# Rounding a quantised activation: the magnitude by a bit mask on VectorE, the subtraction on GpSimd

## What is computed

```python
def _div_clamp_fp8(x, scale):
    y = jnp.clip(x.astype(jnp.float32) / scale, -FP8_MAX, FP8_MAX)   # 448
    y = y.astype(jnp.bfloat16).astype(jnp.float32)
    return _fp8_roundtrip(y)                                          # float8_e4m3fn
def _fp8_linear_pertensor(x, wq, w_scale, in_scale):
    xq = _div_clamp_fp8(x, in_scale)
    return jnp.einsum('bsi,oi->bso', xq * in_scale, wq) * w_scale
...
ln_out = _ln(hidden_states, ln_w, ln_b)
q  = _fp8_linear_pertensor(ln_out, wq,  wq_scale,  q_in_scale)
k  = _fp8_linear_pertensor(ln_out, wk,  wk_scale,  k_in_scale)
v  = _fp8_linear_pertensor(ln_out, wv,  wv_scale,  v_in_scale)
qx = _fp8_linear_pertensor(ln_out, wqx, wqx_scale, qx_in_scale)
```

## Time and profile before

| | |
|---|---|
| median of 3 runs | 1316.26 us (1315.24 to 1320.13) |
| the profiled execution | 1319.29 us, its span 1317.5 us |
| mean granted TensorE clock | 0.986 of full speed |
| busy, share of the span | TensorE 94%, VectorE 84%, ScalarE 75%, GpSimd 54% |
| the chain that ended last | TensorE 75%, VectorE 11%, ScalarE 5%, DMA 3%, GpSimd 2% |
| pieces of the rounding | 32, the first begins at 15.7 us, the last ends at about 135 us |

### The profile page before, as it was taken

How to read it: one execution, slowest core, us unless ns; L and a number is a source line. 1 busy time by engine, 2 the same in 40 slices (tenths; PEclk the granted TensorE clock), 3 DMA queues, 4 the chain that set the end, 5 groups by cost and what they waited for, 6 DMA issues and landing times.

```text
span 1317.5 us, 28707 instructions
## 1 busy us (share of the span) xinstructions
PE 1237.3 (94%) x10612; PEld 1089.1 (83%) x10612; DVE 1100.4 (84%) x2220; ACT 982.3 (75%) x2186; POOL 705.5 (54%) x614
## 2 busy tenths in 40 slices
PE   1688999999999999999999999999999999998998
PEld 1578899999999999999999999987877545555998
DVE  8989879999989999989999988986666768876654
ACT  5799788789987889898789897755433456674775
POOL 5667555656656657556565564433210346664585
PEclk9989999999999999999999999999999999998999
DMA  4222332231132321223321111221186703125762
GB/s 149 83 73 68 97 93 77 75 92 50 56 87 63 96 76 48 71 76 74 89 66 43 34 37 28 75 75 39 29 150 149 148 27 74 47 98 188 254 230 78
DMA packets 117513, 114.02 MB, mean 87 GB/s; under 512 B 12411, under 2 KB 102491, under 8 KB 116768
## 3 DMA queue, kind: packets, MB, share of 16 engines
q1 hardware_dynamic: 115152, 106.11, 29.3%
q0 software_dynamic: 2048, 6.05, 1.3%
q10 hardware_dynamic: 176, 0.04, 0.0%
HBM read 80.20 MB, written 32.00 MB: 85 GB/s over the span
## 4 chain that ended last, share of the span: by engine, by line
PE 75%; DVE 11%; ACT 5%; DMA 3%; issue 3%; POOL 2%; SPq 0%; POOLq 0%; DVEq 0%; ACTq 0%
PE PC L599 8%; PE PO L581 7%; PE SS L565 7%; PE B L542 5%; PE PA L498 4%; PE PA L500 4%; PE B L1319 3%; PE B L1850 2%; PE PA L512 2%; PE PA L511 2%; PE PC L589 2%; PE PA L510 2%; PE PO L1300 2%; PE B L555 2%; PE PA L523 2%
## 5 line engine op out<-in xcount | busy, mean ns | idle before, releaser
L1093 POOL TENSOR_TENSOR RB<-YS,M 128x512 bf16<-128x512 f32 x128 | 162.5, 1270 | 309.7 <-DVE YS L928 309.7
L718 ACT ACTIVATE QT<-B,sm 128x256 f32<-128x256 f32 x256 | 131.9, 571 | 43.5 <-PE B L542 43.4
L498 PE MATMUL PA<-WH,XQ 128*128 128x256 f32 x512 | 140.4, 306 | 17.4 <-DVE WL L874 13.3
L1088 POOL TENSOR_TENSOR yy<-vv,half 128x14 f32<-128x14 f32 (+1 forms) x64 | 148.4, 2318 | 5.3
L565 PE MATMUL SS<-QT,KT 128*128 128x256 f32 x512 | 132.9, 382 | 3.1 <-DVE mx L878 3.1
L500 PE MATMUL PA<-WL,XQ 128*128 128x256 f32 x512 | 129.6, 285 | 0.0
L741 ACT ACTIVATE PPP<-SS 128x512 f32<-128x512 f32 x128 | 77.7, 607 | 68.7 <-PE SS L568 68.6
L898 DVE TENSOR_TENSOR QN<-QN,yy 128x512 f32<-128x512 f32 x128 | 127.1, 993 | 0.8 <-POOL yy L1088 0.8
L890 DVE TENSOR_REDUCE vv<-SQ 128x7 f32<-128x896 f32 (+1 forms) x128 | 120.7, 943 | 0.4 <-ACT SQ L764 0.3
L498 PEld LDWEIGHTS PA<-WH,XQ 128*128 128x128 f32 x512 | 98.7, 193 | 18.9 <-DVE WL L874 13.7
L542 PE MATMUL B<-identf,QN 128*128 128x128 f32 x768 | 106.2, 275 | 2.0 <-ACT LNT L673 1.0
(11 more groups left out here) (369 smaller groups left out, 4148.4 us busy)
## 6 DMA issues: line engine op xcount, KB each, us to landing
W<-in_w SPq DMA_DIRECT2D x16, 1024.0 KB
XK<-xk_d SPq DMA_DIRECT2D x24, 512.0 KB, 4.3
V<-v_d SPq DMA_DIRECT2D x112, 64.0 KB
v_d<-VST SPq DMA_DIRECT2D x48, 128.0 KB, 2.3
Q<-qsc SPq DMA_DIRECT2D x8, 768.0 KB, 10.2
WR<-in_wprojT SPq DMA_DIRECT2D x16, 256.0 KB, 3.0
xk_d<-XK SPq DMA_DIRECT2D x8, 512.0 KB, 3.9
kt_d<-KT SPq DMA_DIRECT2D x64, 64.0 KB, 1.7
```

Source lines behind the costliest of these rows:

```text
L498: pe.matmul(PA[:, 256 * k:256 * k + 256], XQ[:, k, c, bs], wh[:, c, 256 * k:256 * k + 256], start=c == 0, stop=False)
L718: a.activation(QT[i % 2][:, o:o + 256], B1[:, o:o + 256], ACT.Identity, bias=col(n + "b"), scale=col(n + "w"))
L1088: p.tensor_tensor(yy[j % 2][:, :, 0:n], v_, half[:, 0:2 * n].rearrange("p (h k) -> p h k", h=2), ALU.pow).then_inc(s_rstd, 1)
L1093: p.tensor_tensor(RB[i % 2][:], YS[:], M[:], ALU.subtract).then_inc(s_rb, 1)
```

## The change

ScalarE makes only QY, now scaled by `scq`, so `scn` goes, and `s_qm` becomes `s_qy`. VectorE clears the sign bit of QY to get QM, clamps QY in place, bounds QM from both sides, and adds 2^-20 QY to QM. GpSimd subtracts QM from the sum, which leaves the rounded value; it no longer clamps. The final operation of a piece on GpSimd so has two tensor inputs in place of one.

```diff
-        scn = sb("scn", [128, 4, 2])
...
-                    a.wait_ge(s_qm, 8 * q4)
+                    a.wait_ge(s_qy, 8 * q4)
...
-            a.activation(QY[i % 3][:], LNT[:, c], ACT.Copy, scale=scn[:, k, c:c + 1])
-            if i >= 2:
-                a.wait_ge(s_qs, i - 1)
-            a.activation(QM[i % 2][:], LNT[:, c], ACT.Abs, scale=scq[:, k, c:c + 1]).then_inc(s_qm, 1)
+            a.activation(QY[i % 3][:], LNT[:, c], ACT.Copy, scale=scq[:, k, c:c + 1]).then_inc(s_qy, 1)
...
-            v.wait_ge(s_qm, i + 1)
+            v.wait_ge(s_qy, i + 1)
             if i >= 2:
                 v.wait_ge(s_q, i - 1)
-            v.scalar_tensor_tensor(out=s_[:], in0=m[:], scalar=QMIN, in1=y[:], op0=ALU.max, op1=ALU.add).then_inc(*vs.up())
-            v.wait_ge(*vs.at())
-            v.scalar_tensor_tensor(out=s_[:], in0=m[:], scalar=QMIN, in1=s_[:], op0=ALU.max, op1=ALU.subtract).then_inc(s_qs, 1)
+            v.tensor_scalar(m[:].bitcast(U16), y[:].bitcast(U16), 0x7FFF, None, ALU.bitwise_and).then_inc(*vs.up())
+            v.tensor_scalar(y[:], y[:], QMAX, -QMAX, ALU.min, ALU.max)
+            v.wait_ge(*vs.at())
+            v.tensor_scalar(m[:], m[:], QMIN, QMAX, ALU.max, ALU.min).then_inc(*vs.up())
+            v.wait_ge(*vs.at())
+            v.scalar_tensor_tensor(out=s_[:], in0=y[:], scalar=1.0 / TWO20, in1=m[:], op0=ALU.mult, op1=ALU.add).then_inc(s_qs, 1)
...
-                v.tensor_scalar(scn[:, k, :], scq[:, k, :], -1.0, None, ALU.mult).then_inc(*vs.up())
...
-            p.tensor_scalar(dst, QS[i % 2][:], 448.0, -448.0, ALU.min, ALU.max).then_inc(s_q, 1)
+            p.tensor_tensor(dst, QS[i % 2][:], QM[i % 2][:], ALU.subtract).then_inc(s_q, 1)
```

More of the change, by code:

```diff
@@ L227, in build @@
         s_zv = sem("zv")
-        s_qturn, s_lnt, s_qm, s_qs, s_q = (sem(n) for n in ("qturn", "lnt", "qm", "qs", "q"))
+        s_qturn, s_lnt, s_qy, s_qs, s_q = (sem(n) for n in ("qturn", "lnt", "qy", "qs", "q"))
         s_c, s_ch, s_ctx = (sem(n) for n in ("c", "ch", "ctx"))
```

## The result

The changed kernel takes 1328.9 us in the median of 6 runs (1326.4 to 1330.6), the kernel before 1317.0 us beside it (6 runs, 1315.2 to 1320.1): a ratio of 1.0085, with a 95% interval of 1.0068 to 1.0103, or +11.9 us. The forecast was 1326.5 us, +10.2 us.

A forecast was written before the change was run, and what follows sets the result against it. Chain before turn 12: VectorE and GpSimd to 59 us, then mostly ScalarE, with VectorE level and becoming the bound. Terms 2.4 + 1.7 + 2.3 - 0.6 + 4.7 - 0.3 = +10.2 us gave 1326.5 us; 80% range 1314 to 1335.

The forecast's parts named there:

- It passes one for one to the end: Behind turn 11 TensorE has the same work and no idle time, so any shift before turn 12 reaches the end.
- The level costs: Lengths without holds, per piece: VectorE 1.36 us instead of 1.33; GpSimd's subtraction at least 1.147 us instead of 0.608.
- The hold: VectorE standing behind a GpSimd subtraction loses 0.54 us more than before; bounds 0 and 0.86 us.
- To 28.2 us: Before the first projection: GpSimd's longer pieces delay VectorE and share ports with pieces 2 and 3, +2.4 us.
- To 59: From the start to 59 us, through piece 11 and the reload of CR: 2.4, 1.7 and 2.3 us more.
- the four scn products: Four products dropped by the change, each on the chain with 0.07 us: together -0.3 us.
- Turns 3 to 5: Turn 3 +0.6 with VectorE full, turn 4 0, turn 5 -1.2 from ScalarE's two removed instructions: sum -0.6 us.
- the rival of a late GpSimd: GpSimd also becomes a bound, adding 1 to 2 us in each of turns 6, 8 and 10: 1332 us, chance 0.12.
- Turns 6 to 11: VectorE becomes the bound: 2.4 us in turns 7, 9, 11 and 3.4 in 6, 8, 10, less idle time: 4.7 us.
- the prediction's first rival: ScalarE's relief comes through: VectorE stays level, twelve L686 leave the chain, -7.3 us, 1309.0 us; chance 0.09.

## Why the prediction was right

*The bound and the place.* "It passes one for one to the end": 12.4 us at block 12, 11.9 between the medians. The other runs say the same, each with one trace: the sum of squares of block 12 lies 1.8 us earlier than in the kernel before with the one-input form of before, and 7.6, 11.5 and 15.3 later with two inputs in the kernel before, with VectorE's subtraction, and with subtraction and clamp exchanged; the ratios give -2.4, +8.4, +10.4 and +14.9 us. The farthest apart are those of the changed kernel with the sum of squares moved in turns 5 to 11, 13.4 against 10.3. One for one is shown to within some 3 us, not closer.

*The level costs.* VectorE's estimate of 1.36 us a piece holds: in turn 7 the two masks of a pair start 1.33 us apart, 103.45 and 104.78. GpSimd's at least 1.147 us came as 1.152.

*The hold.* "Where VectorE stands behind a subtraction, I take 0.54 us more": measured 1.0 instead of 0.29 where a mask precedes, 0.71 more, nearer to the upper bound of 0.86. Over all pieces it is 0.5 us. The term is right in the sum and a little small per place: 0.16 us of it is what a hold gains by the short instructions, as estimated above. It also falls elsewhere than was said: not the first instruction of a second piece, the mask, but the clamp behind it is held, and so often that its median is 0.72 us and not 0.29.

*To 28.2 us*: +2.4 forecast, +2.4 measured. *To 59*: 6.4 forecast (6.1 with the scn products), CL ended 6.7 later. The -0.3 us for the four scn products did not come: the first statistics start no earlier, since VectorE's reciprocal ahead of them then waits for the transfer of the smoothing factors instead.

*Turns 3 to 5*: forecast -0.6, measured +1.3 (8.0 less 6.7). This is the step that failed: "in turn 5 ScalarE's two removed instructions come through". The three scalings of weights on GpSimd (L1027) took 4.70 us in place of 2.83, with VectorE's rounding of two pieces now beside them, where before only the start of one was; the root behind them came late, and ahead of the scaling of the queries at 82.22 VectorE stood idle for 1.9 us; that scaling was then held for 1.0 by the next subtraction. That is the rival of a late GpSimd, in one turn and at 2 us; I had looked for it in turns 6, 8 and 10.

*Turns 6 to 11*: forecast 4.7, measured 4.4 from turn 6 to block 12 (12.4 less 8.0).

*The rivals.* In the changed kernel ScalarE's relief is worth 0.4 to 1.6 us, far from the 7.3 us that its twelve places on the chain of before suggested. That is no verdict on the 7.3 us in the kernel before. With the one-input form of before the whole is 2 us faster although VectorE's pieces are held 7 us more, and with two inputs in the kernel before, where they are also held 7 us more (17 against 10) but ScalarE has no relief, it is 8 us slower. The distance of 10 us between these two is an upper estimate of what the relief pays as long as VectorE is held for no more than that; they differ also in the length of GpSimd's step. No run has the relief alone, so between 2 and some 10 us its worth there stays open, and the prediction's first rival may have had a real gain in it that the two-input form used up.

The Trainium skill, "SBUF — State Buffer", section on the two separate sides, says that the shared port pair is held for the whole instruction. The subtraction agrees roughly (1.0 us of hold for 1.15), the product with a minimum does not: 0.45 us of hold for 1.92. By the rule that run's pieces would have held VectorE for about as long as GpSimd was busy; the measurement decides. The same clamp L843 was held for 0.45 us by one-input instructions of 0.61 and of 1.92 us and for 1.0 us by the two-input one of 1.15 us, and L848 for 0.29 us by one input and 0.72 by two. So the hold looks more like the tensors read than the length; why, no run shows.

## What to carry to other kernels

Work moved to an engine with idle time is free only if it leaves the bound engine alone: price a GpSimd instruction by what it does to VectorE's instructions beside it, and look for two-input forms in particular. Splitting one long VectorE instruction into short ones gives GpSimd more openings, and the same neighbour then held VectorE for longer (0.45 us instead of 0.29). Where two engines are level, what the relief of one is worth can depend on how far the same change loads the other; a run with the relief alone tells.

## What was not expected of the hardware

- On GpSimd a one-input instruction with a product and a minimum on 128x512 took 1.92 us, with a minimum and a maximum 0.61 us.
- That 1.92 us instruction held VectorE for 0.45 us only, and two further VectorE instructions, one of them with two tensor inputs, ran beside it without a hold. Of all VectorE instructions that began beside one of the 32, none was held for more than 0.47 us.
- VectorE holds GpSimd as well: three scalings of 128x256 on GpSimd went from 2.83 to 4.70 us beside the rounding of two pieces, each of three instructions of 0.28 us and one of 0.69; which of them hold was not measured.
